# Low parts of the values of tiles 12 to 31 made by GpSimd instead of by VectorE in a graph attention kernel

## What is computed

```python
h = jnp.maximum(_layernorm(x, axis=-1), 0.0)
# _L0_gnn_ref:
h = x @ W.T
src = h @ a1
dst = h @ a2
e = jax.nn.leaky_relu(src[:, None] + dst[None, :], negative_slope=ALPHA)
e = jnp.where(adj == 0, jnp.float32(NEG_INF), e)
attention = jax.nn.softmax(e, axis=1)
h_prime = attention @ h
x = x + h_prime
```

## Time and profile before

| | us |
|---|---|
| median of 3 runs | 386.72 (386.38 to 386.8) |
| time of the profiled execution | 385.06 |
| span of the profiled execution | 383.4 |
| TensorE busy | 376.3 |
| VectorE busy | 364.6 |
| ScalarE busy | 195.5 |
| GpSimd busy | 45.1 |

### The profile page before, as it was taken

The page is one execution under the profiler, slowest core; times in us unless marked ns, Lnnn a source line. Parts: engine busy times, 40 slices in busy tenths (PEclk is TensorE's granted clock), DMA queues, the critical chain, the costliest instruction groups (busy, mean ns, idle before and its releaser), DMA issues.

```text
span 383.4 us, 9273 instructions
## 1 busy us (share of the span) xinstructions
PE 376.3 (98%) x3366; PEld 332.1 (87%) x3366; DVE 364.6 (95%) x474; ACT 195.5 (51%) x282; POOL 45.1 (12%) x73
## 2 busy tenths in 40 slices
PE   8999899999999999999999999999999999999996
PEld 6888688888888788888888888888888888888885
DVE  4999999999999999999999999999987999999965
ACT  5899856453353644344445544444446443444330
POOL 3998020000000001110000002100000012100000
PEclk9999999999999999999999999999999999999999
DMA  7920466767567666766666667766655567666403
GB/s 251 367 97 3 146 221 218 239 217 253 188 202 234 207 216 217 238 230 222 218 222 202 219 216 227 242 221 217 223 200 192 166 214 243 227 223 220 165 2 109
DMA packets 26112, 77.95 MB, mean 203 GB/s; under 512 B 2916, under 2 KB 8552, under 8 KB 26088
## 3 DMA queue, kind: packets, MB, share of 16 engines
q1 hardware_dynamic: 24800, 74.46, 58.2%
q0 software_dynamic: 1280, 3.16, 2.2%
q10 hardware_dynamic: 8, 0.00, 0.0%
HBM read 73.40 MB, written 4.21 MB: 202 GB/s over the span
## 4 chain that ended last, share of the span: by engine, by line
PE 74%; DVE 19%; issue 4%; DMA 2%; ACT 1%; ACTq 0%; DVEq 0%
PE ps L1410 66%; DVE p_lo L791 8%; DVE p_sb L784 7%; PE ps L1220 2%; PE ps L1234 2%; PE ps L1245 2%; PE ps L1240 2%; DVE v_sb L756 2%; DMA adj_sb<-adj_t 1%; DVE p_lo L777 1%; DVE p_sb L765 1%; DMA a_rows<-a 1%; DVE rows_sb L1131 0%; ACT hnt_hi L480 0%; PE ps L1191 0%
## 5 line engine op out<-in xcount | busy, mean ns | idle before, releaser
L1410 PE MATMUL ps<-v_sb,p_hi 128*128 (+2 forms) x2048 | 251.6, 273 | 1.9 <-ACT p_hi L501 1.7
L511 ACT ACTIVATE p_hi<-p_sb,gp 128x1024 f16<-128x1024 f32 x126 | 144.4, 1149 | 166.8 <-DVE p_sb L784 139.4
L1410 PEld LDWEIGHTS ps<-v_sb,p_hi 128*128 128x128 f16 x2048 | 199.4, 98 | 27.8 <-issue 2.4
L791 DVE SCALAR_TENSOR_TENSOR p_lo<-p_sb,gp,p_hi 128x1024 f16<-128x1024 f32 x126 | 160.8, 1279 | 7.1 <-ACT p_hi L511 6.6
L784 DVE SCALAR_TENSOR_TENSOR p_sb<-c_row,gp,adj_sb 128x1024 f32<-128x1024 uint32 (+1 forms) x126 | 160.5, 1279 | 0.0
L1410 PE MATMUL ps<-v_sb,p_lo 128*128 (+1 forms) x1024 | 142.6, 273 | 0.0
L1410 PEld LDWEIGHTS ps<-v_sb,p_lo 128*128 128x128 f16 x1024 | 100.1, 98 | 12.6 <-DVE p_lo L791 0.2
L448 POOL DMA_DIRECT2D out<-rows_sb x24 | 13.0, 542 | 264.8 <-DVE rows_sb L1098 264.8
L390 POOL TENSOR_SCALAR hn_sb<-x_sb,moments,rstd 128x256 f32<-128x256 f32 x18 | 22.6, 1263 | 6.7 <-DVE rstd L740 6.1
L750 DVE SCALAR_TENSOR_TENSOR hnt_lo<-ps,hnt_hi 128x256 f16<-128x256 f32 x32 | 13.0, 410 | 0.4 <-ACT hnt_hi L480 0.4
L756 DVE TENSOR_TENSOR v_sb<-h_sb,v_sb 128x256 f16<-128x256 f32 x32 | 13.1, 420 | 0.0
(11 more groups left out here) (81 smaller groups left out, 92.3 us busy)
## 6 DMA issues: line engine op xcount, KB each, us to landing
adj_sb<-adj_t SPq DMA_DIRECT2D x128, 512.0 KB, 4.7
x_sb<-x SPq DMA_DIRECT2D x7, 512.0 KB, 8.3
out<-rows_sb POOLq DMA_DIRECT2D x24, 128.0 KB, 4.6
c_row<-c_flat SPq DMA_DIRECT2D x3, 512.0 KB, 5.6
out<-rows_sb SPq DMA_DIRECT2D x8, 128.0 KB, 1.7
x_sb<-x SPq DMA_DIRECT2D x2, 256.0 KB, 3.7
w_nat<-w SPq DMA_DIRECT2D x1, 256.0 KB, 2.7
w_f<-w_t SPq DMA_DIRECT2D x1, 256.0 KB, 3.9
```

Source lines behind the costliest of these rows:

```text
L511: nc.scalar.activation(p_hi[:, u % R, :], p_sb[:, u % R, :], ACT.Copy, scale=p_scale[:, bass.ds(t, 1)])\
L791: nc.vector.scalar_tensor_tensor(out=p_lo[:, u % R, :], in0=p_sb[:, u % R, :], scalar=p_scale[:, bass.ds(t, 1)], in1=p_hi[:, u % R, :], op ...
L1410: return nc.tensor.matmul(ps[:, k, 0:width], part[:, u % R, k * P:(k + 1) * P], v_sb[:, bass.ds(t, 1), v, 0:width], start=start, stop=stop ...
```

## The change

GpSimd gets a function value_lo of its own, with the same subtraction. It does tiles 12 to 15 before the four stores of c_flat and tiles 16 to 31 after them. Each waits until v_lo_ready has reached t, so that the count still goes up in order of the tiles, and for the tile's high part. The twenty calls of value_lo(12) to value_lo(31) are taken out of VectorE's order, whose other instructions stay as they were.

```diff
--- before.py
+++ after.py
@@ -73,6 +73,7 @@
     KEPT_BY_VECTOR = []
     KEPT_BY_SCALAR = list(range(0, T))
     RN = 8
+    LOW_BY_VECTOR = 12
     RT = 8
 
     HN_UP = 2.0 ** 11
@@ -390,6 +391,12 @@
                 nc.gpsimd.tensor_scalar(hn_sb[:, t % RN, :], x_sb[:, t, :], moments[:, t, 0:1], rstd[:, t:t + 1],
                                         ALU.subtract, ALU.mult).then_inc(hn_gpsimd_ready, 1)
 
+            def value_lo(t):
+                pool.wait_ge(v_lo_ready, t)
+                pool.wait_ge(*high_part_of(t))
+                nc.gpsimd.tensor_tensor(v_sb[:, t, 1, 0:F], h_sb[:, t, 0:F], v_sb[:, t, 0, 0:F], ALU.subtract)\
+                    .then_inc(v_lo_ready, 1)
+
             def value_hi(t):
                 pool.wait_ge(*kept(t))
                 nc.gpsimd.tensor_copy(v_sb[:, t, 0, 0:F], h_sb[:, t, 0:F]).then_inc(v_hi_gpsimd, 1)
@@ -438,9 +445,13 @@
             value_hi(11)
             value_hi(12)
 
+            for t in range(LOW_BY_VECTOR, LOW_BY_VECTOR + R):
+                value_lo(t)
             pool.wait_ge(c_blocks_ready, 1)
             for b in range(P // T):
                 pool.dma_start(c_flat[:, b * T:(b + 1) * T], c_blocks[b * T:(b + 1) * T, :]).then_inc(c_flat_stored, 16)
+            for t in range(LOW_BY_VECTOR + R, T):
+                value_lo(t)
 
             with pool.Fori(0, NG - 1) as g:
                 for k in range(RB):
@@ -991,7 +1002,6 @@
             dve.wait_ge(p_lo_ready, 5)
             edge_weights(0, 8, 48, 0)
             split_lo(7, 7, 0)
-            value_lo(12)
             dve.wait_ge(p_lo_ready, 6)
             edge_weights(1, 9, 48, 0)
             split_lo(0, 8, 8)
@@ -1002,22 +1012,17 @@
...
             edge_weights(5, 29, 128, 0)
             split_lo(4, 28, 24)
-            value_lo(29)
             split_lo(5, 29, 24)
             dve.wait_ge(p_lo_ready, 27)
             edge_weights(6, 30, 128, 0)
-            value_lo(30)
             dve.wait_ge(p_lo_ready, 28)
             edge_weights(7, 31, 128, 0)
             split_lo(6, 30, 24)
-            value_lo(31)
             split_lo(7, 31, 24)
 
             def group_den(g):
```

More of the change, by code:

```diff
@@ L1004, in _ @@
             split_lo(3, 11, 8)
-            value_lo(13)
             dve.wait_ge(p_lo_ready, 9)
@@ L1009, in _ @@
             edge_weights(5, 13, 64, 0)
-            value_lo(14)
-            value_lo(15)
             split_lo(4, 12, 8)
-            value_lo(16)
             dve.wait_ge(p_lo_ready, 11)
@@ L1019, in _ @@
             split_lo(6, 14, 8)
-            value_lo(17)
             dve.wait_ge(p_lo_ready, 13)
@@ L1029, in _ @@
             split_lo(1, 17, 16)
-            value_lo(18)
             dve.wait_ge(p_lo_ready, 16)
@@ L1035, in _ @@
             split_lo(2, 18, 16)
-            value_lo(19)
-            value_lo(20)
             split_lo(3, 19, 16)
@@ L1040, in _ @@
             edge_weights(5, 21, 96, 0)
-            value_lo(21)
             split_lo(4, 20, 16)
-            value_lo(22)
             dve.wait_ge(p_lo_ready, 19)
@@ L1049, in _ @@
             split_lo(6, 22, 16)
-            value_lo(23)
             dve.wait_ge(p_lo_ready, 21)
             edge_weights(0, 24, 112, 0)
-            value_lo(24)
             split_lo(7, 23, 16)
-            value_lo(25)
             split_lo(0, 24, 24)
@@ L1060, in _ @@
             edge_weights(2, 26, 112, 0)
-            value_lo(26)
             split_lo(1, 25, 24)
@@ L1065, in _ @@
             edge_weights(3, 27, 112, 0)
-            value_lo(27)
             dve.wait_ge(p_lo_ready, 25)
             edge_weights(4, 28, 128, 0)
-            value_lo(28)
             split_lo(3, 27, 24)
```

## The result

The changed kernel takes 388.71 us in the median (388.4 to 389.31, 5 runs) beside 386.38 for the kernel before on the same chip: a ratio of 1.0072 (95% interval 1.0058 to 1.0086), or 2.8 us slower (2.2 to 3.3). The forecast was 2.4 us slower. The profiled execution shown here took 389.31, with a span of 387.7.

The account below looks back on a forecast made before the run. TensorE was taken as the bound, fed by VectorE with thin leads. TensorE 3.1 us late at tile 16, less 0.76 recovered at the group's end, gives +2.4 on 386.72: 389.1 us, range 385.9 to 395.0.

Parts of the forecast that it names:

- What bounds the kernel: First group: TensorE sets the pace at 2.63 us a tile, fed by a VectorE that is only just ahead.
- the 0.76: End of the first group: TensorE loses 0.44 us at tile 31 and 0.32 at group 1's first products.
- c: Delay of busy VectorE by each moved subtraction on GpSimd: 0.38 us, bounds 0 and 0.5.
- The checkpoints: Tiles 9 and 16, TensorE's leads 0.14 and 0.15 us: 9c - 0.48 = 2.9 and 14c - 2.19 = 3.1 us late.
- What comes back: End of the first group: VectorE is 2.3 us ahead, so both TensorE losses vanish, -0.76 us.
- The first delay: TensorE in the first group: delayed already at tile 2, then at tiles 9 and 16.
- GpSimd's own time: One moved subtraction on GpSimd: 0.8 us, bounds 0.4 and 1.22; even at 1.22 nothing is late by itself.
- c_flat: Its four stores, behind tiles 12 to 15 on GpSimd: not delayed, still starting at 51.61 us.
- Rival A: GpSimd's reads slip into VectorE's turnarounds, c below 0.22: 385.96 us at c = 0, 387.5 at 0.22; chance 0.35.
- Rival B: GpSimd holds the SBUF port for its whole operation, c = 0.8, TensorE 9.2 us late: 395.9 us; chance 0.08.
- Rival C: GpSimd starves beside VectorE, delaying c_flat's stores and tile 16's edge loads: +11 us, 398; chance 0.10.

Follow-up runs that it names:

- e1_no_input: The changed kernel, but GpSimd writes zeros instead of subtracting, so it reads nothing from SBUF: 385.41 us beside 385.77 for the kernel before, ratio 0.9982.
- e4_added: Also called the added kernel: the kernel before, with GpSimd doing the 20 subtractions besides, into a spare tile: 394.4 us beside 385.77, ratio 1.0215.
- e2_one_input: The changed kernel, but GpSimd casts h, one input, in place of the subtraction: 385.87 us beside 385.77 for the kernel before, ratio 1.0003.
- e5_tiles_12_17: The changed kernel, but GpSimd makes only the low parts of tiles 12 to 17, VectorE the others: 386.89 us beside 386.14 before, ratio 1.0023.
- e6_tiles_18_31: The changed kernel, but GpSimd makes only the low parts of tiles 18 to 31, VectorE the others: 387.6 us beside 386.14 before, ratio 1.004.

## Why the prediction was right

- **What bounds the kernel.** Right. TensorE keeps 2.63 us a tile in all of them where VectorE isn't late, and a VectorE without its subtractions is worth 0.7 us (e1_no_input), the 0.76 read from two rows.
- **The size of c.** 0.38 was doubled from one-input delays of 0.17 and 0.21. The trace of after has 0.38 to 0.41 in single operations, and by VectorE's delay at the end, where its last low part starts at 125.88, (125.88 - 42.98) - (122.47 - 41.60) = 2.0 us (the forecast had 0.8), plus the 6.8 removed, 0.44 for each of 20. Of this 0.5 us in all are five gaps of 0.1 before low parts with no GpSimd operation beside them; the spacings beside GpSimd's give 0.41, and so does the added kernel. The doubling was luck in part: in the first group one input costs 0.14, not 0.19, and two cost nearly three times that. A turnaround of VectorE that swallows some 0.1 us of each read would fit 0.14 and 0.16 for 256 elements, 0.4 for 512 and 0.02 for 28 (an estimate from these four). The 0.13 of the strided 28-column operation and the 0.77 behind the stores don't fit it, and no run tests it.
- **The checkpoints.** With the delays that the spacings show, 3.8 us by tile 9 and 5.8 by tile 16, the sums give 3.8 - 0.48 = 3.3 and 5.8 - 2.19 = 3.6; measured were 3.41 and 3.81. The forecast's 2.9 and 3.1 were low by the size of c, by 0.4 and 0.5, and little else. The measured 3.81 less 0.76 gives 3.0, and 2.9 was measured in the trace.
- **What comes back.** Right: the waits at tile 31 and at group 1's banks are gone.
- **The first delay.** It came sooner than tile 2: tile 0's high products took 2.82 us where they had taken 2.03, and tile 2 started 1.87 late. But part of that is the clock of 1.2 GHz from 44.5 on, at which a product takes 0.42 us instead of 0.27. In e4_added, with the same four early subtractions and the full clock there, they took 2.23 and tile 2 started 1.46 late.
- **GpSimd's own time.** I estimated 0.8 us; it is 0.68 to 1.67, most of it waiting for VectorE's operation to end. As said it is late for nobody.
- **c_flat.** The stores start at 54.45, 2.8 us later, of which 1.4 is the execution's; GpSimd waited for c_blocks there, not the other way round.
- **Rival A** (little contention) is refuted for two inputs of 256 columns, and is what happens with one. **Rival B** (held for the whole operation): the excess is 0.4 beside operations of 1.3 to 1.7, so as a rule VectorE isn't held for all that the profile shows of one. Once it was: 0.77 beside the 0.68 us at 56.69, as much as B's price of 0.8. The Trainium skill's rule (SBUF — State Buffer, section "Who interferes with whom") that beside a VectorE instruction with two SBUF inputs a write-only GpSimd instruction doesn't contend and a reading one does is what e1_no_input and e4_added show, 0 against 0.41 us each. **Rival C** (starving) didn't happen in the changed kernel, but e2_one_input shows that it can.

## What to carry to other kernels

An operation moved from VectorE to an idle GpSimd is not free if both read SBUF at the same time: price it by what it does to the busy engine (here 0.41 us each) against what it took there (0.34 us), before asking whether the idle engine is fast enough. Where a bounding engine is fed with leads of 0.14 us, make the sum at the tightest places, not over the stage, and at every tile: six operations early in the group made TensorE 2.2 us late at tile 9, while VectorE was only 0.7 late by the end (e5_tiles_12_17), and with 14 moved the tightest place was a tile that no list had (e6_tiles_18_31). And when only some of a counted series is moved, look at what the count then waits for.

## What was not expected of the hardware

- GpSimd's reads beside VectorE operations with two inputs cost VectorE 0.14 us for one input of 256 columns, 0.16 for two of 128, 0.38 to 0.41 for two of 256, and a GpSimd write of 256 columns nothing. A piece of 28 columns cost 0.13 with a strided input and two scalars from SBUF, and 0.02 with neither: it isn't only the size that counts.
- The first subtraction behind GpSimd's DMA issues cost 0.77 in place of 0.4, in all three traces that have it.
- GpSimd got in at each end of a VectorE operation for 40 casts on end, and elsewhere one cast was held out for 5.00 us by four undelayed VectorE operations, and the one before it for 2.77 us.
